# Split fp16 products for the user and gate layers, logits in three turns, retrieval sums spread over pairs and steps

## The reference

```python
mask = (sequence_ids != 0)[..., None]
seq_emb = jnp.where(mask, item_embeddings[jnp.clip(sequence_ids - 1, 0)], 0.0)
pooled = seq_emb.sum(axis=1) / jnp.maximum(mask.sum(axis=1), 1)
user_rep = pooled @ W_rec.T + b_rec
retrieved = item_embeddings[retrieved_indices].mean(axis=1)
gate = jax.nn.sigmoid(jnp.concatenate([user_rep, retrieved], axis=1) @ gate_W.T + gate_b)
fused = gate * user_rep + (1.0 - gate) * retrieved
logits = fused @ proj_W.T + proj_b          # 2048 x 12500
```

## Time and profile before

| | |
|---|---|
| median of three runs | 2319.06 us |
| profiled execution | 2322.34 us |
| its span | 2320.6 us |
| TensorE busy (matmul / weight load) | 2137.7 / 1089.6 us |
| VectorE busy | 1491.1 us |
| GpSimd busy | 1142.5 us |
| ScalarE busy | 716.1 us |
| HBM read and written | 416.21 and 136.48 MB |

### The profile page before, as it was taken

How to read it: one execution, slowest core, us unless ns; L and a number is a source line. 1 busy time by engine, 2 the same in 40 slices (tenths; PEclk the granted TensorE clock), 3 DMA queues, 4 the chain that set the end, 5 groups by cost and what they waited for, 6 DMA issues and landing times. The chain is left out here.

```text
span 2320.6 us, 31173 instructions
## 1 busy us (share of the span) xinstructions
PE 2137.7 (92%) x12548; PEld 1089.6 (47%) x12548; DVE 1491.1 (64%) x1701; ACT 716.1 (31%) x947; POOL 1142.5 (49%) x830
## 2 busy tenths in 40 slices
PE   5669999987999989999998978998999999999999
PEld 4545554544545544444443433443444444444444
DVE  8998898866878764462786656876625444444343
ACT  6856775443445442232311111211112110011110
POOL 5673541888648887775488874888400000000000
PEclk9779999999999999999999989999999999999999
DMA  9998995999769999897788885988824544444453
GB/s 305 333 201 277 309 323 200 269 249 239 243 211 241 251 235 386 284 339 241 238 299 294 280 282 181 314 294 284 281 85 155 173 165 159 173 164 158 160 173 111
DMA packets 205197, 554.76 MB, mean 239 GB/s; under 512 B 20992, under 2 KB 104192, under 8 KB 201728
## 3 DMA queue, kind: packets, MB, share of 16 engines
q0 software_dynamic: 77632, 218.16, 34.5%
q1 hardware_dynamic: 74624, 232.21, 28.8%
q10 hardware_dynamic: 52800, 102.41, 11.9%
HBM read 416.21 MB, written 136.48 MB: 238 GB/s over the span
## 5 line engine op out<-in xcount | busy, mean ns | idle before, releaser
L950 PE MATMUL pooled_ps<-mid,ring 128*128 128x512 f16 x3136 | 740.6, 385 | 18.9 <-DVE mid L581 7.9
L437 POOL DMA_INDIRECT gathered<-emb,ret_rows x452 | 570.8, 1263 | 215.1 <-issue 132.0
L950 PEld LDWEIGHTS pooled_ps<-mid,ring 128*128 128x128 f16 x3136 | 296.1, 99 | 338.8 <-issue 46.1
L743 DVE SCALAR_TENSOR_TENSOR ring<-pooled_ps,out_scale,counts 128x500 f32<-128x500 f32 x320 | 235.3, 736 | 340.4 <-PE pooled_ps L1023 336.0
L1023 PE MATMUL pooled_ps<-counts,keys 128*128 128x500 f16 x1920 | 426.9, 379 | 28.8 <-DVE ring L743 22.8
L459 POOL DMA_INDIRECT gathered<-emb,ret_rows x184 | 343.9, 1869 | 143.7 <-DVE keys L558 80.0
L1023 PE MATMUL pooled_ps<-counts,mid 128*128 128x500 f16 x1920 | 411.8, 374 | 0.0
L556 DVE TENSOR_TENSOR row_hots<-pair_columns,keys 128x2048 f16<-128x2048 f16 x256 | 312.7, 1222 | 76.2 <-PE count_ps L932 75.4
L932 PE MATMUL count_ps<-keys,row_hots 128*128 128x98 f16 x4096 | 281.7, 225 | 84.9 <-DVE keys L558 69.4
L598 DVE TENSOR_TENSOR gathered<-gathered 128x1024 f32<-128x1024 f32 x196 | 240.4, 1227 | 171.5 <-DMA gathered<-emb,ret_rows 157.6
L932 PEld LDWEIGHTS count_ps<-keys,row_hots 128*128 128x128 f16 x4096 | 251.4, 107 | 166.1 <-DVE keys L558 83.9
(11 more groups left out here) (96 smaller groups left out, 1017.3 us busy)
## 6 DMA issues: line engine op xcount, KB each, us to landing
logits<-ring ACTq DMA_DIRECT2D x100, 1000.0 KB, 6.1
ring<-emb_parts SPq DMA_DIRECT2D x147, 512.0 KB, 5.9
counts<-proj_t SPq DMA_DIRECT2D x50, 1000.0 KB, 5.6
counts<-emb SPq DMA_DIRECT2D x14, 1792.0 KB, 10.6
mid<-emb SPq DMA_DIRECT2D x49, 512.0 KB, 7.6
emb_parts<-ring SPq DMA_DIRECT2D x49, 512.0 KB, 6.6
counts<-proj_b SPq DMA_DIRECT2D x50, 250.0 KB, 3.6
gathered<-emb,ret_rows POOLq DMA_INDIRECT x652, 5.9
```

The costliest lines, as they stand in the source:

```text
L437: pool.indirect_dma_start(slots[group][:, a], None, source, column(block, r * SLOT + a))\
L743: dve.scalar_tensor_tensor(rows[:, r % ROW_SLOTS, v], logit_ps[n % BANKS][:, 0:W], out_scale[:, t % 2, j // 4:j // 4 + 1], bias[:, t % 2], ...
L950: last = pe.matmul(pooled_ps[:, m], ring_v[:, p % RING, c, part, m * P:(m + 1) * P], cvt[:, p % CVT, c], start=(i == 0 and c == 0 and part ...
```

## The change

1. User and gate products from fp16 parts: weights, pooled sums, user vectors and retrieved vectors are split into high and low parts (sum of squares, scale, high on ScalarE, low on VectorE); a product over one k slice is three fp16 matmuls. The raw weights are loaded after pair 4 of pass 3, both together; the pooled sums of group 0 wait for the weights' low parts.
2. For groups 0 and 1 transposes come first. All places are new; group 1's scale and parts fall into the first two logits steps.
3. The strips are gone through three times: 8 steps each for groups 0 and 1, 4 each for group 2, 4 each for group 3, still 400 steps, but 75 strips instead of 50 to load and split.
4. Adds: `(0, 26, 52, 126)` by pass instead of `(0, 34, 68, 140)`, then two per three steps instead of one per step. In pass 3 VectorE waits, before the adds of pair i, until pair i - 1 is pooled. GpSimd's lane turns and stores move to earlier indices, and the slot order of the first batches changes.
5. Start: three high parts come earlier on ScalarE; `make_recip(0)` moves to pair 8 of pass 0, the address chain of blocks 2 to 15 to pair 10, the sums of lanes 0 and 1 from pass 1 to pairs 36 and 38 of pass 0.

```diff
-PIECES_PASS = {0: (7, 8, ..., 18), 1: (27, ..., 38)}
-PIECES_LOGITS = {2: (58, 60, ..., 77), 3: (102, 104, 106, 108, 163, ..., 174)}
+FIRST_TURN = [(kind, m) for kind in (TURN, USER, GATE) for m in range(KH)]
+ORDER = {0: FIRST_TURN, 1: FIRST_TURN, 2: FIRST_USER, 3: FIRST_USER}
+PASS = {
+    0: dict(pool=10, pieces=(8, 9, 10, 11, 12, 13, 14, 15, 22, 23, 24, 25), square=16, sum=17, high=19, low=20,
+            mix=27, fsum=29, flow=30),
+    1: dict(pool=33, pieces=(33, 33, 34, 34, 35, 35, 36, 36, 42, 43, 44, 45), square=37, sum=38, high=40, low=40,
+            mix=46),
+}
+LOGITS = {
+    1: dict(fsum=0, flow=1),
+    2: dict(pool=96, pieces=(100, 102, 104, 106, 112, 113, 114, 115, 124, 126, 128, 130), square=117, sum=119, high=120,
+            low=122, mix=132, fsum=137, flow=139),
+    3: dict(pool=150, pieces=(152, 154, 156, 158, 256, 257, 258, 259, 268, 270, 272, 274), square=261, sum=263, high=264,
+            low=266, mix=276, fsum=281, flow=283),
+}
+WEIGHTS = dict(square=(3, 4), sum=5, high=(6, 7), low=(6, 7))
-ADDS_PASS = (0, 34, 68, 140)
+ADDS_PASS = (0, 26, 52, 126)
...
+    STEPS = [(t, j) for t in range(3 * NS) for j in range(8 if t < NS else 4)]
-            return min(len(pl.adds), ADDS_PASS[NG - 1] + max(0, n - 3))
+            return min(len(pl.adds), ADDS_PASS[NG - 1] + max(0, n - 3) * 2 // 3)
...
             def load_pool(g):
-                    sp.wait_ge(gate_used, g)
+                    sp.wait_ge(fused_low, g)
+                else:
+                    sp.wait_ge(weight_low, 2)
...
-                        if i == 5:
+                        if i == 4:
+                            sp.dma_start(raw_rec, ...); sp.dma_start(raw_gate, ...)
+                        if i == 14:
                             load_pool(0)
-                        if i == 29:
+                        if i == 36:
                             load_pool(1)
...
-                if index == 4:                  # store_lane(0), store_lane(1)
+                if index == 3:
-                    if index == 6 + 2 * turn:   # gather_lane(2, turn)
+                    if index == 3 + 2 * turn:
-                    if index == 46 + 2 * turn:  # gather_lane(3, turn)
+                    if index == 34 + 3 * turn // 2:
-                if index == 44 / 80:            # store_lane(2) / store_lane(3)
+                if index == 33 / 59:
-                if index == 82 / 126 / 214:     # load_ret(0) / (1) / (2)
+                if index == 61 / 110 / 212:
...
+                    if g == NG - 1 and i > 0:
+                        wait_pair(dve, g * NP + i - 1)
...
+            def split_products(to, weights, high, low, m, first, last):
+                for k in range(KH):
+                    for at, (w, x) in enumerate(((0, high[k]), (0, low[k]), (1, high[k]))):
+                        done = pe.matmul(to, weights[:, w, k, m * P:(m + 1) * P], x, start=..., stop=...)
+            def sum_weights():
+                wait_sums_read("weight")
+                pe.wait_ge(weight_squared, 2)
+                pe.matmul(spare_ps[:, 8:10], ones_f[:], weight_sq, ...).then_inc(weight_summed, 1)
+            def high_weight(w):                 # ScalarE
+                act.wait_ge(weight_scaled, 1)
+            def low_weight(w):                  # VectorE
+                dve.wait_ge(weight_high, w + 1)
+            def high_pool(g):                   # ScalarE
+                act.wait_ge(pool_in, 16 * (g + 1))
...
                 if j == 0:
                     pe.wait_ge(strip_low, t + 1)
-                if j % 4 == 0:
-                    pe.wait_ge(fused_low, 2 * half + j // 4 + 1)
+                if j % GROUP_BLOCKS == 0:
+                    pe.wait_ge(fused_low, g + 1)
```

More of the change, by code:

```diff
@@ L92, in place_batches @@
         free = deque((group, None) for group in range(LANES * lane, GROUPS))
+        free += [(group, ("lane", 1)) for group in range(lane, LANES * lane)]
         free.append((GROUPS, ("low",)))
-        free += [(group, ("lane", 1)) for group in range(lane, LANES * lane)]
         late = deque()
@@ L125, in pooling_program, with ended, group_of_step @@
     NS, W = pl.strips, pl.width
-    HALF_BLOCKS = NB // 2
-    LAST = 2 * NS * HALF_BLOCKS
+    GROUP_BLOCKS = G // P
+    TURNS = 3 * NS
+    STEPS = [(t, j) for t in range(TURNS) for j in range(2 * GROUP_BLOCKS if t < NS else GROUP_BLOCKS)]
+    LAST = len(STEPS)
+    def ended(t):
+        return sum(1 for turn, j in STEPS if turn <= t)
+    def group_of_step(t, j):
+        return j // GROUP_BLOCKS if t < NS else t // NS + 1
     with ExitStack() as scope:
@@ new lines, in dense_step @@
+            def dense_step(at, places):
+                if places is PASS:
+                    if WEIGHTS["sum"] == at:
+                        scale_weights()
+                    for w in range(2):
+                        if WEIGHTS["low"][w] == at:
+                            low_weight(w)
+                for g, place in places.items():
+                    if place.get("pool") == at:
+                        low_pool(g)
+                    if place.get("sum") == at:
+                        scale_both(g)
+                    if place.get("low") == at:
+                        low_both(g)
+                    if place.get("mix") == at:
@@ L981, in dense_piece, with wait_sums_read @@
+                    split_products(to, w_gate[:, :, 0:KH], high, low, m, True, False)
+                    high, low = [ret_high[:, k] for k in range(KH)], [ret_low[k // 2][:, k % 2] for k in range(KH)]
+                    last = split_products(to, w_gate[:, :, KH:2 * KH], high, low, m, False, True)
                 last.then_inc(dense_made, 1)
-            def wait_sums_read(strips, groups):
+            sums_made = {"weight": 0, "both": 0, "fused": 0, "strip": 0}
+            def wait_sums_read(kind):
@@ L984, in wait_sums_read @@
                 pe.wait_ge(recip_made, NG)
[L985 to L988 removed]
+                if sums_made["weight"] > 0:
+                    pe.wait_ge(weight_scaled, sums_made["weight"])
+                if sums_made["both"] > 0:
+                    pe.wait_ge(both_scaled, sums_made["both"])
+                if sums_made["fused"] > 0:
+                    pe.wait_ge(fused_scaled, sums_made["fused"])
```

331 lines of the change are left out of this document (216 added, 115 removed).

## The result

The changed kernel takes 2228.8 us (median of five runs, 2227.0 to 2232.8), the kernel before on the same chip 2320.0: a ratio of 0.9605, 95% interval 0.9589 to 0.9621, 91 us faster. The forecast was 2192 us in a range of 2155 to 2240. The direction was right, the time is 37 us above the forecast and in the range. Ratios leave out the executions in a slower state of the chip: one of e3's six (3642 us), and nine of the 17 of the kernel before beside e5 to e8 (2370 us and more; the other eight took 2332 to 2365).

What follows compares the result with a forecast made beforehand. TensorE was taken as the bound after the first 155 us, with idle time besides. Pass 0 -2, pass 1 -27.5, pass 2 -16, pass 3 +1.5, logits -83 sum to -127 from 2320.6: 2193.6, median 2192 us, range 2155 to 2240.

Steps and rivals of the forecast that it cites:

- Passes 1 and 2: With 26 adds each, slower than GpSimd's batches, the stalls should go: 27.5 and 16 us gained.
- rival 2: Gathers stay the pace: half the stalls of passes 1 and 2 and of the logits remain, 2234 us; chance 0.17.
- Dense products: User and gate pieces from fp16 parts take 2.59 and 5.17 us, saving 20.4 us in pass 3 and in the logits.
- net gain of 2 us: Pass 0: moving both chains off the front gains slightly more than they and the lane sums cost; bounds 12 and -3.
- 11 to 12 us: Front of pass 0: gain from the 7.75 us hole, 3.4 us at half clock and 1.4 us at the first pair.
- near pair 9: Pass 3: a TensorE hole of about 10 us, ended by a widening behind the rec high part.
- the pass loses 22 us: Pass 3: holes, half-clock time and waits for low parts, against 20.4 us saved, net +1.5.
- bounds of 0 to 30: Pass 3's loss: 0 if batches land calmly and the holes close, 30 us if each step comes late.
- Rival 1: Pass 3: the weight chain closes in time, keeping its 20 us and some of pass 0's front, 2165 us; chance 0.22.
- step of the adds: Logits: one add per 1.5 steps, 3.8 us, is slower than GpSimd's 3.1 us.
- I take 12 us lost: Logits: time still lost, of 75 us before, so the gain is 63 + 20.4 = 83 us.
- The rule beside it: Pass 3: 21 us of new VectorE conversions slow gathers by 6 us, or up to 21 by the port rule, near 2207.

Runs made afterwards that it cites:

- e3: Changed kernel with make_recip(0) back at pair 0 and the address chain back ahead of pass 0: 2229.2 us, ratio 0.9592.
- e5: Changed kernel with group 2's sum of squares and parts 3 logits steps later, group 3's mix 2 and sum and parts 3 later: 2239.3 us, ratio 0.9542.
- e8: Changed kernel with e2, e3 and e5 combined, lanes 2 and 3 summed at pair 38 of passes 1 and 2, adds (0, 28, 57, 126): 2251.3 us, ratio 0.9601.
- e4: Changed kernel with adds (0, 34, 57, 126), lanes 2 and 3 summed at pair 38 of passes 1 and 2: 2233.4 us, ratio 0.9604.
- e11: Changed kernel with e3 and e5, adds (0, 28, 55, 126), lane 3 summed at pair 42 of pass 2: 2212.4 us, ratio 0.9525.
- e10: Changed kernel with every second gather of a retrieved row replaced by a plain read of the same size: 2219.9 us, ratio 0.9572.
- e7: Changed kernel with one add per logits step instead of two in three steps: 2335.8 us, ratio 0.9926.
- e6: Changed kernel with only the product of the two high parts in the dense products: 2190.6 us, ratio 0.9324.
- e1: Changed kernel with lane 3 summed at pair 42 of pass 2 instead of pair 1 of pass 3: 2231.3 us, ratio 0.9600.
- e2: Changed kernel with VectorE's dense step ahead of the pair's adds in pass 3: 2234.8 us, ratio 0.9623.
- e9: Changed kernel again, unaltered, on the chip of the last three runs: 2233.4 us, ratio 0.9622.

## Why the prediction was right, and where it was not

**Passes 1 and 2: right, to a microsecond, and the cause shown for most of pass 1.** 28.7 and 16.6 us went where 27.5 and 16 were forecast. The reason given, more adds than GpSimd's gathers can feed, is shown for 17 of the 28.7: e4 brings these back in pass 1 with eight adds more, and e8 and e11 add 11 and 5.6 us to pass 2 with three and one more. Nothing is left of rival 2 here; that gathers stay the pace came true in pass 3 instead.

**Dense products: right.** 2.59 and 5.18 us a piece for 2.59 and 5.17.

**Pass 0: the net gain of 2 us was 7 of loss.** The cost side held: the pairs of the two chains lost 4.7 and 4.1 us, the lane sums 0.8 and 1.2, 10.8 for 10.3. The term that failed is "11 to 12 us" for the hole: pairs 2 to 5 took 22.7 us against 27.1 in the kernel before and 29.3 in e3, only 4.4 to 6.6, and the first pair gained nothing (6.4 us for 5.6). I took the hole away without asking what is late next; ScalarE's 11.2 us of waits for embedding rows show it. Both chains were paid in full, for about half of the gain.

**Pass 3: the mechanism right, its length too short.** The hole "near pair 9", the widening behind the rec high part, the adds ahead of it and the wait at pair 12 all came, at 878.9 and 902.5 us for some 880 and 902. The term "the pass loses 22 us" was 29.5. The two holes of the forecast with their half-clock time cost a little less than priced, 18 us over clean pairs (pairs 8 and 9, and 12); 12 us more stand at pairs 29 and 30 (5) and 33 and 34 (7), which had no place in my sum. I worked out GpSimd's times only up to batch 63 and let the pace of 3.1 us per batch against 3.6 us per add clear the backlog unnamed. e10 shows that it doesn't: less GpSimd time per batch gave 18.9 us; e4 and e11 agree (both with lane 3 earlier: five adds fewer 15.8, three fewer 15.3). The 5 us at pairs 29 and 30 are another thing: the sum of squares comes two pairs after the mix, whose three operations take VectorE 7 us, and GpSimd's pace does not move it. The bounds of 0 to 30 held, barely. Rival 1 was wrong for this reason.

**Logits: the largest miss, one term.** The step of the adds was right (e7: 67 to 89 us hang on it), and so were the piece times and, but for group 3's mix, the feed of the strips. "I take 12 us lost" was 34: 24 us of gaps, and 8.5 for the 16.9 us that TensorE works at 1.2 GHz beside them. I had priced group 3's mix and high parts (5 us; the gap there was 6.7, and 2 more for the clock) and loads (3 to 7), but not group 2's sum of squares at 137, nor the strip sums, nor the clock. e5 takes 8.0 of them by three steps of delay; the rest, 3.2 us twice at low parts and 2.6 twice at a strip's sum, was not tried.

**The rule beside it: it holds, at under half its price.** The timelines of VectorE and of GpSimd in pass 3 of the changed kernel show a low part of the gate weights and the gather issued during it:

```profile
882.50 4.48 DVE L721 SCALAR_TENSOR_TENSOR counts<-counts,keys 128x4096 f16<-128x4096 f32 x1 [0.27 <-ACT counts L918]
...
883.35 4.45 POOL L496 DMA_INDIRECT gathered<-emb,ret_rows  x1 [0.30 <-issue]
888.11 1.01 POOL L496 DMA_INDIRECT gathered<-emb,ret_rows  x1 [0.30 <-issue]
```

A gather that meets no VectorE operation takes 0.95 us. This one lasts until 0.82 us after the low part's end, and so it is with the adds: of 146 plain gathers issued during one, 137 ended 0.80 to 0.84 us after it. 83 gathers issued during an eviction (L858), which reads PSUM, took 0.94 to 0.97 us all the same. The estimate of 2207 rests on the Trainium skill (SBUF — State Buffer, "Who interferes with whom"), by which GpSimd and a VectorE operation that takes the shared port pair exclude each other for the whole instruction; the trace agrees, for gathers and operations with both inputs in SBUF, with 4.45 us beside 4.48. The price was too high: the time beyond 0.95 us a gather came to 35.6 us in pass 3 against 27.4 before, 8.8 of it behind the new conversions, so some 8 us where the slope gave 6 and the rule up to 21. The result is nearer to 2207 than to 2192, but most of the miss lies in the holes above. What I missed is that the adds hold the gathers that they wait for: 18.0 of the 35.6 us.

**What stays open**: whether pairs 3 to 5 of pass 0 could be fed by earlier loads, how much of e6's pass 3 was that chip, which move beside the adds took 12 us out of pass 1, and whether slower adds would do as well with two turns.

## What to carry to other kernels

Where two engines in series feed a third, price the pace of the slowest over the whole stage and not only up to the first stall: a hole that closes at one pair comes back at the next place that needs the same late engine (e1 and e2 against e10). Slowing an off-path task can be the gain: adds at two per three steps instead of one per step are worth 67 to 89 us here, because an in-order engine can't evict while it waits. Before moving work into a full stretch, name what is late behind the hole that it leaves.

## What the hardware showed unexpectedly

- The lock above holds a gather but not a plain DMA issued by GpSimd: the 86 of pass 3 in e10 took 0.557 us on average and at most 0.57, whether VectorE worked or not.
- In e10 a gather cost GpSimd 1.408 us on average against 1.194 in e9, so half plain reads saved only 28.8 of 162.4 us of its work on these buffers (95.7 + 37.9). The time beyond 0.95 us is much the same in both (35.2 and 39.1 us in pass 3) and falls on half as many gathers.
- On the chip of e5 to e8 TensorE falls into stretches in which a matmul comes only every 0.7 to 1.4 us with no releaser named, between 921 and 985 us above all (pairs 14 and 15 of e5 take 24.4 us for 12.0). VectorE stands for up to 17.4 us and ScalarE for up to 23.3, both with a releaser that the trace names remote, while GpSimd goes on issuing gathers and the packets of its queue go on finishing. Why is open. One such window of e5, columns as in the earlier trace rows:

```profile
925.00:930.00 5.00, 2.34 (x5) 0.45 (x4) 0.00 (x0) 1.72 (x2) 3.78 (x5) 0.78 0.75 229
```

- Passes 1 and 2 with 26 adds repeat within 4 us from chip to chip (218.2 to 221.8, most of it at the first pair, which takes 3.4 to 6.3 us), while pass 0 with the moved chains varies between 236 and 242.
